# A transformer layer loop: output turns ahead of the Wo product, V projected in full tiles and laid out by DMA, the feed-forward loop written out

## The reference

```python
for i in range(6):                       # 16 heads of 64, window 32, INNER = 1024
    q, k, v = split(shift_tokens(x) @ Wqkv[i])
    q, k = l2norm(q) * qs, l2norm(k) * ks   # then rotary tables, k with the inverse scale
    out = local_attention(q, k, v)       # each window of 32 queries sees its own 32 keys
                                         # and the 32 before it; softmax over 64 slots
    x = out @ Wo[i] + x
    x = (a * gelu(gate)) @ W2[i] + b2[i] + x   # a, gate = split(layer_norm(shift_tokens(x)) @ W1 + b1)
```

## Time and profile before

| what | us |
|---|---|
| median of 3 runs | 5136.06 |
| the runs | 5130.78 to 5147.4 |
| the profiled execution: its own time | 5136.26 |
| its span (first to last instruction) | 5134.4 |
| layer 1, attention with prologue | about 549 (1894 to 2443) |
| layer 1, feed-forward | about 92 (2443 to 2535) |

### The profile page before, as it was taken

One profiled execution on the slowest core, in us unless ns is written; L12 is line 12 of the kernel. 1 busy time (PEld: TensorE's weight loads), 2 busy tenths in 40 slices (PEclk: granted clock), 3 DMA queues, 4 the chain that ended last, 5 costly groups with the idle time before them and its releaser, 6 DMA issues. The chain is left out here.

```text
span 5134.4 us, 182125 instructions
## 1 busy us (share of the span) xinstructions
PE 4374.8 (85%) x70227; PEld 2980.5 (58%) x70227; DVE 3356.9 (65%) x7024; ACT 2441.1 (48%) x5161; POOL 2570.1 (50%) x4541
## 2 busy tenths in 40 slices
PE   8999946765899888998889988999889998899985
PEld 6777733653566545666456664666546665466653
DVE  3555533365777657776577765777667776677765
ACT  3555543222555535554355543555435554355542
POOL 0000000001777627776277762777627776277761
PEclk9999968887999999999999999999989999899998
DMA  1000001201111111111111111111111111011111
GB/s 37 5 4 4 2 1 50 58 6 48 32 32 32 25 30 32 32 32 25 30 32 32 32 25 30 32 32 32 26 29 32 32 32 30 25 32 32 32 24 33
DMA packets 76107, 143.17 MB, mean 28 GB/s; under 512 B 19654, under 2 KB 57748, under 8 KB 68116
## 3 DMA queue, kind: packets, MB, share of 16 engines
q1 hardware_dynamic: 75284, 131.92, 10.5%
HBM read 35.40 MB, written 4.19 MB: 8 GB/s over the span
## 5 line engine op out<-in xcount | busy, mean ns | idle before, releaser
L2437 DVE TENSOR_TENSOR n_tt<-n_pp,n_rot 128x1024 f32<-128x1024 f32 x768 | 922.2, 1220 | 615.7 <-ACT n_sq L2307 615.5
L1939 POOL TENSOR_TENSOR n_pre<-n_tt 128x512 f32<-128x512 f32 x768 | 964.1, 1278 | 288.6 <-DVE n_tt L2437 288.2
L2055 PE MATMUL n_pp<-n_wqkv,n_xT 128*128 128x512 f32 x1536 | 794.9, 620 | 10.6 <-ACT n_xT L2302 10.4
L1974 POOL TENSOR_TENSOR n_pre<-n_pre,n_rn 128x512 f32<-128x512 f32 x768 | 777.6, 1045 | 34.2 <-POOL n_rn L1962 34.2
L2307 ACT ACTIVATE n_sq<-n_pp 128x512 f32<-128x512 f32 x768 | 459.3, 598 | 596.8 <-PE n_pp L2055 595.2
L2444 DVE TENSOR_REDUCE n_ss<-n_sq 128x8 f32<-128x512 f32 x768 | 518.5, 675 | 0.0
L2329 ACT ACTIVATE n_E<-n_E 128x512 f32<-128x512 f32 x384 | 235.7, 630 | 582.1 <-DVE n_E L2456 582.1
L2072 PE MATMUL n_pp<-ident,n_pre 128*128 128x128 f32 x3072 | 417.5, 278 | 51.3 <-POOL n_pre L1974 50.6
L2072 PEld LDWEIGHTS n_pp<-ident,n_pre 128*128 128x128 f32 x3072 | 359.2, 144 | 172.1 <-issue 93.5
L2318 ACT COPY n_qkT<-n_pp 128x512 f32<-128x512 f32 x768 | 421.5, 603 | 61.7 <-PE n_pp L2072 60.1
L2086 PE MATMUL n_pp<-n_wo,n_OT 128*128 128x128 f32 x3072 | 403.3, 285 | 8.8 <-ACT n_OT L2324 4.9
(11 more groups left out here) (263 smaller groups left out, 8240.9 us busy)
## 6 DMA issues: line engine op xcount, KB each, us to landing
n_Vx<-n_V SPq DMA_DIRECT2D x192, 256.0 KB, 3.9
n_Vx<-n_V SPq DMA_DIRECT2D x192, 192.0 KB, 3.6
n_wqkv<-in_L_ffn_Wqkv SPq DMA_DIRECT2D x6, 1536.0 KB, 6.5
e_w<-in_L_ffn_w SPq DMA_DIRECT2D x32, 256.0 KB, 3.0
m_Y<-e_ye SPq DMA_DIRECT2D x64, 64.0 KB, 2.0
n_wo<-in_L_ffn_Wo SPq DMA_DIRECT2D x6, 512.0 KB, 7.3
a_xs<-in_L_attn_x SPq DMA_DIRECT2D x16, 128.0 KB, 2.1
x_kept<-X SPq DMA_DIRECT2D x1, 2048.0 KB, 8.3
```

The source lines that it names most:

```text
L1939: nc.gpsimd.tensor_tensor(d, s[0], s[1][:, :, ::-1, :], ALU.add).then_inc(s_add, 1)
L1974: nc.gpsimd.tensor_tensor(d, d, bcast(rn[:, j, t, 8 * half:8 * half + 8], 2, D), ALU.mult).then_inc(s_kn, 1)
L2055: nc.tensor.matmul(pp[:, c % 2, :], xT[:, j * P:(j + 1) * P], wqkv[:, t * I + 512 * half:t * I + 512 * half + 512], start=True, stop=True) ...
L2437: nc.vector.tensor_tensor(tt[:, c % 4, :, :].rearrange("p s (h d) -> p s h d", d=D), bcast(pp[:, c % 2, :].rearrange("p (h d) -> p h d", d ...
```

## The change

Four edits, all in `l1_network`.

1. **Order.** In each half, PE does the two output turns before the Wo product; the turn of the weights moves behind the first q/k turn. ACT copies the two turned outputs before the exponentials, and the first turned q/k before the weights. `SHARED` follows: v, v, o, o, y.
2. **V.** A call of `project_v` is one product with 128 tokens of stationary and 512 output columns. ACT copies it into a new tile `Vn` (one buffer, tokens on partitions). DMAs of SP then fill both `V` and `Vx` from `Vn`: ten when the first half's two copies are done, eight after the second's; 18 a sequence, in pieces of 512 bytes. ACT's V copies wait until the 18 DMAs of the sequence before have landed, as `Vn` has one buffer.
3. **Buffers.** `E` and `On` have one buffer in place of two; DVE's writes wait for the turns of the half before.
4. **Feed-forward.** The four pairs of groups are written out, with no `Fori`.

```diff
-    SHARED = ([("v", 0, 1), ("v", 1, 1), ("y", 0, -1), ("o", 2, -1), ("o", 3, -1)] + [("turn", 4 + r, 0) for r in range(4)]
-              + [("v", 2, 1), ("v", 3, 1), ("y", 1, -1), ("o", 0, 0), ("o", 1, 0)]
+    SHARED = ([("v", 0, 1), ("v", 1, 1), ("o", 2, -1), ("o", 3, -1), ("y", 0, -1)] + [("turn", 4 + r, 0) for r in range(4)]
+              + [("v", 2, 1), ("v", 3, 1), ("o", 0, 0), ("o", 1, 0), ("y", 1, -1)]
...
-            pair(0, True, False)
-            with eng.Fori(1, NG // 2 - 1) as i:
-                pair(i, False, False)
-            pair(NG // 2 - 1, False, True)
+            for i in range(NG // 2):
+                pair(i, i == 0, i == NG // 2 - 1)
...
-                        after(sp, s_V, 4 * N + 4)
-                        for f in range(2):
-                            lo, hi = 64 * f, 64 * f + W
-                            sp.dma_start(Vx[lo:lo + W, u, 1:4, :], V[hi:hi + W, u, 0:3, :]).then_inc(s_vx[u], 16)
-                            sp.dma_start(Vx[hi:hi + W, u, :, :], V[lo:lo + W, u, :, :]).then_inc(s_vx[u], 16)
+                        for j in range(NT):
+                            after(sp, s_V, 4 * N + 2 * j + 2)
+                            for f in range(2):
+                                lo, hi = 64 * f, 64 * f + W
+                                own = Vn[:, j, :].rearrange("p (c f n) -> p f c n", c=4, f=2)[:, f, :, :]
...
+                                place_v(V, lo, 2 * j, own[0:64, :, :])
+                                place_v(V, lo, 2 * j + 1, own[64:P, :, :])
+                                place_v(Vx, hi, 2 * j, own[0:W, :, :])
+                                place_v(Vx, lo, 2 * j + 1, own[W:P - W, :, :])
+                                if j == 0:
+                                    place_v(Vx, lo, 2, own[P - W:P, :, :])
...
-                wv = wqkv[:, 2 * I:3 * I].rearrange("p (c f n) -> p f c n", c=4, f=2)
-                for f in range(2):
-                    last = nc.tensor.matmul(pp[64 * f:64 * f + 64, bank, :].rearrange("p (c n) -> p c n", c=4),
-                                            xT[:, 64 * m:64 * m + 64], wv[:, f, :, :], start=True, stop=True)
+                nc.tensor.matmul(pp[:, bank, :], xT[:, j * P:(j + 1) * P],
+                                 wqkv[:, 2 * I + 512 * half:2 * I + 512 * half + 512],
+                                 start=True, stop=True).then_inc(s_v, 1)
...
                     scores(j)
-                    if prev:
-                        output(N - 1, j, bank("y", j, -1))
                     if j == 1:
                         turn_output(N, 0, bank("o", 0, 0))
                         turn_output(N, 1, bank("o", 1, 0))
...
-                    turn_weights(N, j)
+                    if prev:
+                        output(N - 1, j, bank("y", j, -1))
                     d = j
                     if nxt or not d:
                         turn_qk(N + d, 4 - 4 * j, bank("turn", 4 - 4 * j, d))
+                    turn_weights(N, j)
+                    if nxt or not d:
                         turn_qk(N + d, 5 - 4 * j, bank("turn", 5 - 4 * j, d))
...
-            def copy_v(N, u, m, bank):
+            def copy_v(N, u, m, bank, pair):
                 after(act, s_PV, 4 * (N - 1))
+                after(act, s_vx[1 - u], 288 * (pair + u))
                 after(act, s_v, 4 * N + m + 1)
-                nc.scalar.copy(V[:, u, m, :], pp[:, bank, :]).then_inc(s_V, 1)
+                nc.scalar.copy(Vn[:, m // 2, 512 * (m % 2):512 * (m % 2) + 512], pp[:, bank, :]).then_inc(s_V, 1)
```

More of the change, by code:

```diff
@@ L1763, in l1_network @@
         qkT = sb("qkT", [P, 2, I // P, T])
+        Vn = sb("Vn", [P, NT, I])
         V = sb("V", [P, 2, 4, 512])
         Vx = sb("Vx", [P, 2, 4, 512])
-        E = sb("E", [P, NT, 2, 512])
+        E = sb("E", [P, 2, 512])
         ET = sb("ET", [P, 2, 4, P])
@@ L1793, in l1_network @@
         s_clear = sem("cleared", False)
-        s_vx = [sem(f"v_shifted{u}", False) for u in range(2)]
+        s_vx = [sem(f"v_placed{u}") for u in range(2)]
         s_xs = sem("x_staged")
@@ L2060, in project_v @@
                 after(pe, s_xT, N + 1)
-                wv = wqkv[:, 2 * I:3 * I].rearrange("p (c f n) -> p f c n", c=4, f=2)
-                for f in range(2):
-                    last = nc.tensor.matmul(pp[64 * f:64 * f + 64, bank, :].rearrange("p (c n) -> p c n", c=4),
-                                            xT[:, 64 * m:64 * m + 64], wv[:, f, :, :], start=True, stop=True)
-                last.then_inc(s_v, 1)
+                j, half = m // 2, m % 2
+                nc.tensor.matmul(pp[:, bank, :], xT[:, j * P:(j + 1) * P],
+                                 wqkv[:, 2 * I + 512 * half:2 * I + 512 * half + 512],
+                                 start=True, stop=True).then_inc(s_v, 1)
             def turn_qk(N, r, bank):
@@ L2078, in turn_output @@
                 for c in range(4):
-                    last = nc.tensor.transpose(pp[:, bank, c * P:(c + 1) * P], On[:, j, f, c * P:(c + 1) * P],
+                    last = nc.tensor.transpose(pp[:, bank, c * P:(c + 1) * P], On[:, f, c * P:(c + 1) * P],
                                                ident[:, :])
@@ L2117, in turn_weights @@
                     for c in range(4):
-                        last = nc.tensor.transpose(pW[:, e, c * P:(c + 1) * P], E[:, j, e, c * P:(c + 1) * P],
+                        last = nc.tensor.transpose(pW[:, e, c * P:(c + 1) * P], E[:, e, c * P:(c + 1) * P],
                                                    ident[:, :])
@@ L2139, in weights_ready @@
                 if j == 0:
-                    after(pe, s_V, 4 * N + 4)
-                    pe.wait_ge(s_vx[u], 64 * (pair + 1))
+                    after(pe, s_vx[u], 288 * (pair + 1))
             def prologue(N, l):
@@ L2328, in exps @@
                 after(act, s_sub, 4 * N + 2 * j + e + 1)
-                nc.scalar.activation(E[:, j, e, :], E[:, j, e, :], ACT.Exp).then_inc(s_E, 1)
+                nc.scalar.activation(E[:, e, :], E[:, e, :], ACT.Exp).then_inc(s_E, 1)
             def copy_weights(N, j, e):
@@ L2343, in prologue @@
                     elif kind == "v":
-                        copy_v(N, 0, c, bank)
+                        copy_v(N, 0, c, bank, l * (NB // 2))
                     else:
@@ L2357, in attention @@
                         square(N + 1, 4 * j + 1)
-                        copy_v(N + 1, 1 - u, 2 * j, bank("v", 2 * j, 1))
-                        copy_v(N + 1, 1 - u, 2 * j + 1, bank("v", 2 * j + 1, 1))
-                    exps(N, j, 0)
-                    exps(N, j, 1)
+                        copy_v(N + 1, 1 - u, 2 * j, bank("v", 2 * j, 1), pairs[0] + u)
+                        copy_v(N + 1, 1 - u, 2 * j + 1, bank("v", 2 * j + 1, 1), pairs[0] + u)
                     if j == 1:
@@ L2367, in attention @@
                         copy_output(N - 1, 3, bank("o", 3, -1))
+                    exps(N, j, 0)
+                    exps(N, j, 1)
+                    if nxt or not j:
+                        copy_qk(N + j, 4 - 4 * j, bank("turn", 4 - 4 * j, j))
                     copy_weights(N, j, 0)
@@ L2370, in attention @@
                     if nxt or not j:
-                        copy_qk(N + j, 4 - 4 * j, bank("turn", 4 - 4 * j, j))
                         copy_qk(N + j, 5 - 4 * j, bank("turn", 5 - 4 * j, j))
@@ L2412, in feed_forward, with on_pair @@
                 groups(act, l, ff_one)
-            layers(act, attention, feed_forward, prologue)
+            pairs = [None]
+            def on_pair(i):
+                pairs[0] = i
+            layers(act, attention, feed_forward, prologue, on_pair=on_pair)
         @block.vector
@@ L2469, in norm_output @@
                 after(dve, s_ri, 2 * N + j + 1)
-                after(dve, s_OTp, 4 * (N - 1) + 2 * j + 2)
+                after(dve, s_OTp, 4 * N + 2 * j)
                 after(dve, s_PV, 4 * N + 2 * j + 2)
```

13 lines of the change are left out of this document (8 added, 5 removed).

## The result

The changed kernel takes 5071.89 us (median of 4 runs, 5068.13 to 5078.03) against 5134.97 for the kernel before, run beside it (5130.78 to 5147.4). The ratio is 0.9874, 95% interval 0.9855 to 0.9894: 63 us faster, where 104 were forecast. Its profiled span is 5070.2 us.

The account below looks back on a forecast made before the run. The prediction took PE as the bound, POOL close behind; the order saves 17.6 us a layer, 105 in six, V, buffers and feed-forward nothing: 5136.3 - 105 = 5031, taken as 5032 us, range 4975 to 5128.

Parts of the forecast that it names:

- rival (a): Whole kernel, the forecast itself: PE's wait goes and POOL becomes the bound; 5000 to 5070 us, chance 0.66.
- The wait for X goes, the Wo product waits for ACT: Attention halves on PE: 0.97 us wait for DVE's addition goes, 0.35 us wait for ACT's copy of the turned output comes.
- POOL becomes the bound at 31.3 a sequence: Steady attention: POOL's floor 30.65 plus 0.65 of waits gives 31.3 us a sequence; PE needs 31.2.
- The order, 17.6 us a layer: Edit 1 in attention: 15.7 us from 14 sequences plus 1.9 from the last sequence and the first, 105 in six layers.
- In between lie the first q/k turn ... and the weights' turn: Before the second q/k turn on PE: these turns, 0.44 and 0.87 us, exceed the addition's 0.97 lateness, so the wait goes.
- V on PE: "nothing changes", bound 20 us: V products on PE, edit 2: no change in time; bounds 0.1 us either way a half, 20 us in all.
- The transfers hidden: SP's 18 V DMAs a sequence: bursts of 8.0 and 7.0 us fit within a half of 15.6; price nothing.
- Rival (d): SP's queue becomes the bound: at 1.85 us an issue, 34.0 us a sequence, 144 us more, 5280; chance 0.12.
- Buffers nothing: Edit 3, DVE's writes: the turns they wait for are some 10 us old when asked for, so no cost.
- Feed-forward nothing: Edit 4, feed-forward loop: groups already 9.14 us apart across the jump back, so writing it out is worth nothing.
- the forecast's 1.9: Ends of a layer's attention: the last sequence gains 0.62 us in two halves, the first in one; 1.9 us a layer.

Follow-up runs that it names:

- e_newton_before: The kernel before with two refinement steps of the inverse norms on POOL in place of three: 5120.67 us, ratio 0.9972.
- e_newton_after: The changed kernel with two refinement steps of the inverse norms on POOL in place of three: 4947.45 us, ratio 0.9626 to the kernel before.
- e_order: The kernel before with edit 1 alone (order of PE, of ACT's copies and of the shared banks): 5103.35 us, ratio 0.9931.
- e_order_tw: The kernel before with only the output turns moved ahead of the Wo product, weights' turn and its copies left in place: 5048.23 us, ratio 0.9825.
- e_tw_all: The changed kernel with the weights' turn ahead of the first q/k turn in every half, on PE and ACT: 5030.8 us, ratio 0.9798 to the kernel before.

## Why the prediction was right and wrong

The time fell inside the range, and in the steady part the mechanism was the forecast one, though 5071.89 lies just above the 5000 to 5070 that rival (a) gave itself: 63 us came of the 104. The main term, the order, brought far less than it was given, and an edit priced at nothing made up for a part of that, so the total is nearer than its terms. By its own steps:

- **The wait for X goes, the Wo product waits for ACT.** Right: 0.97 a half is gone, 0.29 came (0.35 forecast).
- **POOL becomes the bound at 31.3 a sequence.** Right: 31.36 in layer 1, 31.45 over six. e_newton_before and e_newton_after show the change of bound. That 31.3 was met so closely is in part luck: POOL waited 0.92, not 0.65, and by the same subtraction its own need is 31.36 - 0.92 = 30.44, not 30.65. The two errors cancel.
- **The order, 17.6 us a layer.** This is the term that was mis-sized; it measured 6.1 (e_order), and 14.2 when the weights' turn kept its place (e_order_tw; 15 by the medians). The step that failed is "In between lie the first q/k turn ... and the weights' turn": it added up their durations, which don't depend on their order, and priced the move on ACT as a delay that nobody reads. It didn't ask what PE does while POOL makes the first multiplication. The weights' turn was the work that filled that wait. Moved behind it, it costs 4 us in each layer's opening, where PE's stop is 1.91 us longer, a second one of 2.60 follows, and the clock is lower for longer: 229 us at its lower level from the first copy of xT to the last feed-forward sum of the six layers, 187 before, 184 in e_order_tw and e_tw_all; the first two intervals alone make 50 of it, and 9 before. In the steady part it costs 0.2 to 0.3 us a sequence. The prediction had the first sequence gain 0.6 us with the others, and gave the opening no loss.
- **V on PE: "nothing changes", bound 20 us.** Wrong by its own bound: alone it is worth 39 us (32 to 46), with the single buffers. The error was to compare a pair of V products with a pair of q/k products from their starts. That leaves out the product *before* the change of form, whose successor can't load its weights early. After the change the V edit is worth less, since POOL is the bound: e_order_tw to e_tw_all is 0.27% of the time, 14 us (3 to 25 by both intervals), loop included.
- **The transfers hidden.** Right: no wait for a landing, bursts of 9.1 and 7.9 us at the median against 8.0 and 7.0 forecast. Rival (d) stayed away, at some 17 us of 31.4. With 36 transfers it begins to show: V copies wait for landings 31 times. The slowest issue before was also not the 1.85 us that (d) went by, but 2.29, on L1915.
- **Buffers nothing.** No wait of DVE for the turns of the half before appears among the waits after; this edit was not run by itself.
- **Feed-forward nothing.** Groups 9.14 as forecast. 1 us is saved at the step to the next layer; it isn't shown by which edit.

Summed, a layer: 17.6 us forecast, 10.9 measured, made of 14.2 gained by the output turns, 8.1 lost by the weights' turn and 4.8 gained by the rest (differences of the table's sums). Of the 6.7 missing, the opening makes 5.1 (4.5 lost where 0.6 of the forecast's 1.9 was due), the 26 steady intervals 3.3 (11.3 gained for 14.6) and the end of attention 0.6 (1.8 for 2.4); the first stretch and the step to the next layer, which the forecast left at nothing, give 2.3 back. Left open: how the V edit and the order share what each gives alone (35 and 39 us, 63 together with the loop's 7); POOL's floor caps them, but the split by cause wasn't taken further. How the 4 us of an opening divide between PE's longer stops and the lower clock isn't shown either.

## What to carry to other kernels

When a step is moved in an engine's list, ask what it was filling: the slot that it leaves may have been the cover for another engine's work, and the place where this shows first is the opening of a loop, where the other engine is late. Move the step in every list that carries it, or in none. When an edit changes the form of a product, measure from the product ahead of it to the one behind it, not just the product itself; and where a change bundles edits, run them alone, since here one part of one edit was worth more (90 us) than all four together (63). When a transfer is to be hidden, look for the wait of whoever reuses its buffer: 36 transfers fitted the sequence by their issues alone, and still held up the V copies.

## What the runs showed of the hardware

- A weight load of 64 columns behind products of 128 columns started only with its own product (0.95 us after the load before); a load of the same form started 0.43 us after it. It cost 0.09 us at each change of form (0.52 against 0.43 us from one product's start to the next), and the same stands after the change between V and the scores' small tiles (1434.39, 0.94 us after the last V load).
- Behind a stop of 2.76 us in the opening PE was granted 0.72 of its clock over 6 us, behind one of 4.67 us 0.56, and eight transposes took 1.92 us there in place of 1.04.
- SP issued transfers of 32 or 64 x 2 KB in pieces of 512 bytes every 0.68 us at the median, some issues taking up to 2.16 us; the bursts were limited by this, each transfer landing 2.5 us after its issue at the median. With 36 a sequence the issues filled 27.5 of 31.6 us.
